# Expert stage over a list of 71 slot tiles, with weights addressed through a register, stationary tokens and three places for weights

## Chip, cores and metric

The kernel runs on one core of one Trainium2 chip. The metric is the time of one execution on the device, in microseconds (us), as the median of several runs.

## What is computed

4096 tokens (16 sequences of 256) of 512 features pass two gated residual blocks. The first is a recurrence over time (WKV) with the normalized tokens as keys and the context as values. The second is a mixture of experts: 8 routed experts, two for each token, and one shared MLP of hidden size 1408. The routed part:

```python
logits = x_flat @ router                       # (4096, 8)
topk_logits, sel = jax.lax.top_k(logits, 2)
cw = softmax(topk_logits)
C = 1280                                       # slots of one expert
buf[e, position of the token among those of e] = x_flat[token]    # if the position is below C
gate, up = split(einsum('ecd,edm->ecm', buf, w_up_gate), [352])   # 512 -> 2 x 352
h = silu(gate) * up
out_buf = einsum('eci,eid->ecd', h, w_down)                       # 352 -> 512
y[token] += cw * out_buf[e, position]
out = x + tanh(g_ffn) * (y + shared_mlp(x_flat))
```

Products are made in float16 with each operand split in a high and a low half, so one product is three matmuls (high x high, high x low, low x high).

## The kernel before, in words

Each engine has its own instruction stream, written out in order, and semaphores tie them together. The program has 16 *units* of 256 tokens (two tiles of 128). A unit runs in 11 steps, one for each of the 11 blocks of the shared MLP's hidden size: `up_pair` (matmuls at L930) makes the block's up projection, and `down_block` (L951) the down projection of the unit before. The attention part of later tokens is spread over the same steps by the table `STAGE_AT`: transposes on TensorE (L854), scans and reciprocals on VectorE, factors on GpSimd. Units 1 to 12 run partly in hardware loops, units 12 to 15 are written out. Each step's hidden block goes through one of three buffers (`srng`, and `PU` in PSUM), so TensorE can be three blocks ahead of VectorE. The down projections of units 13 to 15 are *held*: they run on TensorE around the expert stage (`held_down`, L1054), the first half of unit 13's ahead of it and the rest behind.

Routing runs on VectorE beside the units. `send_slots` on GpSimd (L545) writes, by indirect DMA, token number and weight of each choice into the slot table `slot_d` (10240 slots: 8 experts of 1280). The last two routes (`LAST`) come in unit 15: VectorE's `address_slots` for the last one waits (ahead of L1254) until the slots of the one before have been sent. GpSimd then reads the table back (L607), TensorE turns it (`turn_table`), and VectorE makes index lists from it (`slot_indices`, L1201 to L1203).

The expert stage then goes over all 80 slot tiles of 128 slots, filled or not, expert by expert, in *chunks* of two tiles (5 chunks for each expert), in hardware loops over pairs of experts:

- GpSimd copies an expert's indices (L617, L618), gathers the rows of each tile from `xhl_d` (L627) and, when a tile's result is staged, adds it to `moe_d` in memory by an indirect DMA with addition (L645, the scatter-add). Up to two of these are in flight; `retire` (L635) lets a staging buffer go when one has landed.
- SyncE turns gathered rows by DMA transposes (L421) and loads the next expert's weights in 11 pieces (L408, L412).
- TensorE: `up_chunk` (L1018) holds a 128 x 128 (or 128 x 96) block of weights still and streams 256 tokens, 72 matmuls for a chunk; `down_chunk` (L1032) holds tokens' hidden values still and streams 512 weight columns, 9 matmuls for a tile. The up projection of the next chunk is issued ahead of the down projection of this one.
- ScalarE: silu (L813), high half of the hidden block (L815), staging of the result with its weight (L822), high half of the next expert's weights (L800, L803). VectorE: product (L1356), low half (L1359), low half of the weights (L1344, L1348).

Two sets of weight buffers are used in turn, one in `wkv` (free after the attention part), one in `acc`. Expert 0's weights are loaded and split in unit 15. At the end SyncE waits for the scatter-adds, loads the sums of the held tiles, and copies the rest of `moe_d` to the output.

## Time and profile before

| | us |
|---|---|
| median of 3 runs | 1300.6 (1297.64 to 1302.33) |
| the profiled execution | 1298.67 |
| its span, first to last instruction | 1296.9 |
| TensorE matmuls busy | 1222.8 |
| GpSimd, VectorE, ScalarE busy | 667.9, 687.7, 542.0 |
| granted TensorE clock, mean share of full speed | 0.997 |

The profile is of one execution. PE is TensorE's matmuls, PEld its weight loads, PEldq its sequencer, DVE VectorE, ACT ScalarE, POOL GpSimd, SPq SyncE's queue. A matmul's printed duration holds the pipeline's depth as well, so a rate is read from the starts, or from how long many take together. The span starts with the first instruction; 1.8 us of the execution's time lie around it.

### The profile page before, as it was taken

What the parts mean: (1) busy time and instruction counts of PE and PEld (TensorE: products, weight loads), DVE (VectorE), ACT (ScalarE), POOL (GpSimd) and SP (SyncE); (2) the same over time, 40 slices, a digit from 0 to 9 for tenths busy, and PEclk for the clock granted to TensorE, in tenths of its full rate; (3) what the DMA queues carried; (4) which work ended last, traced back from release to release, by engine and by line L of the source; (5) the groups of instructions that cost most, each with busy time, mean ns of one, the idle gap of its engine ahead of it and who ended that gap; (6) DMA issues with size and microseconds to landing.
All of it is one profiled execution on the core that took longest, in us unless ns stands there. A gap on an engine that the chain in (4) does not pass through costs nothing.

```text
span 1296.9 us, 27395 instructions
## 1 busy us (share of the span) xinstructions
PE 1222.8 (94%) x9541; PEld 932.1 (72%) x9541; DVE 687.7 (53%) x1410; ACT 542.0 (42%) x1022; POOL 667.9 (52%) x765
## 2 busy tenths in 40 slices
PE   1579999999999999999999879999999999999998
PEld 1467777777777777777777757777777777777753
DVE  6778767777776766767768533322323232232212
ACT  5676435445344444434444423333434343343320
POOL 7888565474574573664567422444444444444320
PEclk9999999999999999999999989999999999999999
DMA  9272222122131221222111256998988888898748
GB/s 240 72 211 54 63 56 60 49 56 57 57 73 49 63 50 57 57 57 62 45 42 50 41 128 145 163 173 163 176 165 184 152 186 159 166 166 171 122 55 308
DMA packets 188148, 142.74 MB, mean 110 GB/s; under 512 B 127581, under 2 KB 151157, under 8 KB 187936
## 3 DMA queue, kind: packets, MB, share of 16 engines
q1 hardware_dynamic: 167168, 99.38, 31.5%
q0 software_dynamic: 20064, 42.19, 18.0%
q8 instruction: 56, 0.92, 0.3%
q14 instruction: 28, 0.23, 0.1%
q10 hardware_dynamic: 832, 0.02, 0.0%
HBM read 72.19 MB, written 46.81 MB: 92 GB/s over the span
## 4 chain that ended last, share of the span: by engine, by line
PE 79%; DMA 4%; DVE 3%; issue 3%; POOL 1%; ACT 1%; SPq 1%; DVEq 0%; POOLq 0%; ACTq 0%
PE PU L930 28%; PE PU L1018 22%; PE PD L951 14%; PE PD L1032 10%; PE PT L854 2%; DMA wkv<-in_L_ffn_w_up_gate 2%; SPq L421 1%; DMA moe_d<-acc 1%; PE PR L854 1%; POOL slot_d L545 1%; PE PT L1054 1%; PE PR L1054 1%; DMA acc<-moe_d 1%; DVE wkv L1153 1%; DVE srng L1188 0%
## 5 line engine op out<-in xcount | busy, mean ns | idle before, releaser
L930 PE MATMUL PU<-xT,wreg 128*128 128x256 f16 x4224 | 500.4, 273 | 3.7 <-DVE srng L1188 3.7
L930 PEld LDWEIGHTS PU<-xT,wreg 128*128 128x128 f16 x4224 | 410.8, 98 | 73.5 <-DVE srng L1188 3.2
L645 POOL DMA_INDIRECT moe_d<-acc x80 | 129.0, 1612 | 178.0 <-ACT acc L822 144.0
L951 PE MATMUL PD<-wreg,hreg 128*128 128x512 f16 x858 | 206.4, 379 | 0.0
L736 ACT ACTIVATE srng<-PU 128x256 f32<-128x256 f32 x176 | 67.0, 381 | 265.9 <-PE PU L930 243.7
L1018 PE MATMUL PU<-acc,wkv 128*128 128x256 f16 (+1 forms) x1440 | 163.1, 274 | 9.6 <-DMA acc<-xT 6.3
L1018 PEld LDWEIGHTS PU<-acc,wkv 128*128 128x128 f16 (+1 forms) x1440 | 146.9, 107 | 27.8 <-issue 8.4
L1018 PE MATMUL PU<-acc 128*128 128x256 f16 (+1 forms) x1440 | 160.9, 273 | 3.0 <-DVE acc L1356 3.0
L1018 PEld LDWEIGHTS PU<-acc 128*128 128x128 f16 (+1 forms) x1440 | 146.3, 106 | 19.1 <-DVE acc L1356 3.6
L561 POOL TENSOR_TENSOR hreg<-srng,hreg 128x256 f16<-128x256 f32 x165 | 123.0, 749 | 67.6 <-ACT hreg L752 66.2
L951 PEld LDWEIGHTS PD<-wreg,hreg 128*128 128x128 f16 x858 | 84.0, 98 | 73.5
L1188 DVE SCALAR_TENSOR_TENSOR srng<-PU,srng 128x256 f32<-128x256 f32 x176 | 73.9, 420 | 100.4 <-ACT srng L736 97.5
L1356 DVE SCALAR_TENSOR_TENSOR acc<-PU,acc 128x256 f32<-128x256 f32 (+1 forms) x120 | 50.4, 420 | 120.4 <-ACT acc L813 120.3
L1153 DVE RECIPROCAL wkv<-wkv 128x512 f32<-128x512 f32 x32 | 106.9, 3341 | 0.1
L752 ACT ACTIVATE hreg<-srng 128x256 f16<-128x256 f32 x176 | 71.9, 408 | 66.6 <-DVE srng L1188 65.0
L822 ACT ACTIVATE acc<-PD,acc 128x512 f32<-128x512 f32 x80 | 54.8, 685 | 70.9 <-PE PD L1032 41.9
L813 ACT ACTIVATE acc<-PU 128x256 f32<-128x256 f32 (+1 forms) x120 | 45.0, 375 | 88.8 <-PE PU L1018 87.1
L1032 PE MATMUL PD<-acc,wkv 128*128 128x512 f16 (+1 forms) x360 | 81.1, 379 | 0.9 <-ACT acc L822 0.9
L1359 DVE TENSOR_TENSOR wkv<-acc,wkv 128x256 f16<-128x256 f32 (+1 forms) x120 | 51.0, 425 | 57.9 <-ACT wkv L815 50.6
L1032 PE MATMUL PD<-wkv 128*128 128x512 f16 (+1 forms) x360 | 81.1, 379 | 0.0
L545 POOL DMA_INDIRECT slot_d<-stw,sidx x64 | 66.7, 1043 | 25.5 <-issue 15.8
L854 PE MATMUL PT<-ident,wkv 128*128 128x128 f32 x256 | 41.9, 289 | 40.2 <-ACT wkv L700 29.0
(140 smaller groups left out, 1364.0 us busy)
## 6 DMA issues: line engine op xcount, KB each, us to landing
wkv<-in_L_ffn_w_up_gate SPq DMA_DIRECT2D x64, 176.0 KB
acc<-in_x SPq DMA_DIRECT2D x32, 256.0 KB, 3.0
wkv<-in_ctx SPq DMA_DIRECT2D x32, 256.0 KB, 2.7
xhl_d<-wkv SPq DMA_DIRECT2D x32, 256.0 KB, 2.2
moe_d<-acc SPq DMA_DIRECT2D x13, 512.0 KB, 4.4
out<-moe_d SPq DMA_DIRECT2D x2, 3328.0 KB, 21.1
acc<-n_L_ffn_shared_w_up_gate SPq DMA_DIRECT2D x16, 256.0 KB, 5.7
wkv<-in_L_ffn_w_down SPq DMA_DIRECT2D x16, 256.0 KB
```

The costliest lines, as they stand in the source:

```text
L545: pool.indirect_dma_start(out=slot_d, out_offset=bass.IndirectOffsetOnAxis(ap=sidx[:, 2 * t + k:2 * t + k + 1], axis=0), in_=stw[:, k, t, ...
L561: pool.tensor_tensor(hh[:, u.par, m, 1, :], srng[:, r, :], hh[:, u.par, m, 0, :], ALU.subtract).then_inc(hlo_ready, 1)
L645: pool.indirect_dma_start(out=moe_d, out_offset=bass.IndirectOffsetOnAxis(ap=eidx[:, p, 1, s:s + 1], axis=0), in_=ostage[s % 2], in_offset ...
L736: act.activation(srng[:, r, :], PU[r][:, 0:UN], ACT.Silu, scale=1.0 / WS).then_inc(silu_done, 1)
L752: act.activation(hh[:, buf, m, 0, :], srng[:, r, :], ACT.Copy).then_inc(hhi_ready, 1)
L854: mm = pe.transpose(dst[:, kt * P:(kt + 1) * P], src[:, kt * P:(kt + 1) * P], ident[:, :])
L930: mm = pe.matmul(PU[r][:, gu * UN:(gu + 1) * UN], sU[:, m, gu, a, kt, :], xT[:, u.par, b, kt, :], start=(kt == 0 and a + b == 0), stop=(kt ...
L951: mm = pe.matmul(PD[t][:, :], hh[:, u.par, j, a, t * P:(t + 1) * P], sD[:, j, b, :], start=(j == 0 and a + b == 0), stop=(j == JT - 1 and ...
L1018: mm = pe.matmul(PU[r][0:M, gu * CH:(gu + 1) * CH], eU[p][:, gu, a, kt, m * P:m * P + M], xgT[:, (p + j) % 2, b, kt, :], start=(kt == 0 an ...
L1032: mm = pe.matmul(PD[t][:, :], eh[0:M, (p + j) % 2, m, a, t * P:(t + 1) * P], eD[p][0:M, m, b, :], start=(m == 0 and a + b == 0), stop=(m = ...
L1153: dve.reciprocal(nd[:, 1], nd[:, 1]).then_inc(rcp_done, 1)
L1188: dve.scalar_tensor_tensor(out=srng[:, r, :], in0=PU[r][:, UN:2 * UN], scalar=HS / WS, in1=srng[:, r, :], op0=ALU.mult, op1=ALU.mult).then ...
```

## The change

The slot tiles of the expert stage are no longer the 80 of the slot table but a list of 71 positions (8192 choices / 128 + 7). Each expert's filled tiles come at the next free positions, not before a fixed earliest one (`START`), which leaves the remaining experts their room. Unfilled positions gather a valid row and add to rows behind the tokens.

- **Making the list.** GpSimd prepares tables in `place_tables`, after its last `hidden_lo` and before the last `send_slots`. In unit 15 TensorE counts the choices (`count_all`), VectorE computes the places in 8 small dependent steps (`place_tiles`), TensorE moves each position's weight place (*home*) into a row (`place_homes`), VectorE finishes with three more (`place_experts`), and `turn_table` multiplies the slot table with the 0/1 matrix `Pm` where it had been transposed.
- **Weights.** Three homes in `acc`, expert e in home e % 3. TensorE loads the position's home from SBUF into a register (`home_at`) and addresses the weights by it. Expert 0's weights are loaded and split in unit 13, expert 1's in unit 15, the others' during the stage through four buffers (they were two), at fixed positions (`chunks_at`).
- **Up projection.** For one tile at a time the tokens are held still and 352 weight columns stream (24 matmuls). The hidden tile then has tokens in its partitions, so TensorE transposes it in three f32 transposes (`turn_hidden`), issued behind 8 matmuls of the next tile's up projection. ScalarE and VectorE make both halves from the transposed tile, one instruction each. The down projection stays at 9 matmuls of 512 columns.
- **Gather and scatter.** Indices are read where they are, without copies. A scatter-add waits until the one before has landed; three staging buffers (they were two).
- The stage is written out, without hardware loops.

```diff
+NPOS = NTOK * TOPK // P + E - 1
+START = [max(0, NPOS - ET * (E - e)) for e in range(E)]
+HOMES = 3
+EARLY = 2
+EARLY_UNIT = 13
+SMALL = 9728
...
-        ebuf = [wkv[:, 0:EW // 2].bitcast(F16), acc[:, 0:EW // 2].bitcast(F16)]
-        eU = [b[:, 0:UW].rearrange("p (g h k c) -> p g h k c", g=2, h=2, k=KT) for b in ebuf]
-        eD = [b[:, UW:EW].rearrange("p (j h c) -> p j h c", j=IT, h=2) for b in ebuf]
+        home = acc[:, 0:HOMES * EW // 2].bitcast(F16).rearrange("p (n c) -> p n c", n=HOMES)
+        eU = [home[:, n, 0:UW].rearrange("p (g h k c) -> p g h k c", g=2, h=2, k=KT) for n in range(HOMES)]
+        eD = [home[:, n, UW:EW].rearrange("p (j h c) -> p j h c", j=IT, h=2) for n in range(HOMES)]
...
+        ostage = [carve(D) for _ in range(3)]
...
+        def chunk_home(w):
+
+            if w < EARLY * WCH:
+                return w % 2, 16 * (w // 2 + 1)
+            n = w - EARLY * WCH
+            return 2 + n % 4, 16 * (n // 4 + 1)
+
+        def chunks_at(t):
+
+            n, m = divmod(t - 1, ET)
+            if not 0 <= n < E - EARLY:
+                return []
+            return [(n + EARLY, q) for q in range(WCH) if (q // 2 if q < 6 else q - 3) == m]
+
...
-            def turn_slots(e, p, j):
-                cc = EC * e + j
-                for t in range(2):
-                    r = (2 * (EC * p + j) + t) % 4
-                    wait_alone(gathered[r], 16 * (EC * pair_of(e, p) + (2 * (EC * p + j) + t) // 4 + 1))
-                    if not (isinstance(e, int) and cc < 2):
-                        wait_alone(eup_ready, IT * (cc - 1))
-                    sp.dma_start_transpose(
-                        xgT[:, (p + j) % 2, :, :, t * P:(t + 1) * P].rearrange("p h k t -> p (h k) t"), xg[r]).then_inc(turn_done(e, p, j, t)[0], 16)
+            def turn_slots(t):
+                sp.wait_ge(gathered[t % 4], 16 * (t // 4 + 1))
+                if t >= 4:
+                    wait_alone(eup_ready, t - 3)
+                sp.dma_start_transpose(xgT[:, t % 4].rearrange("p h k t -> p (h k) t"), xg[t % 4]).then_inc(xg_turned[t % 4], 16)
...
+            for t in range(NPOS):
+                if t + 4 < NPOS:
+                    turn_slots(t + 4)
+                for e, q in chunks_at(t + 2):
+                    load_chunk(e, q)
+
...
+            def place_tables():
+                ready = [0]
+
+                def keep(ins):
+                    ready[0] += 1
+                    ins.then_inc(cmade, 1)
+                    pool.wait_ge(cmade, ready[0])
+
+                pool.wait_ge(moe_started, 16 * EARLY_PARTS)
+                keep(pool.memset(sel, 1.0))
...
+                keep(pool.iota(own_tile[:, 0:E], pattern=[[ET, E]], base=0, channel_multiplier=-1,
...
+                for e in range(E - 2, -1, -1):
+                    keep(pool.affine_select(out=home_of, in_=home_of, compare_op=ALU.is_ge, fill=float(e % HOMES),
+                                            base=-ET * (e + 1), pattern=[[0, 1]], channel_multiplier=1))
+                for e in range(E):
+                    pool.memset(earliest[:, e:e + 1], float(START[e])).then_inc(cmade, 1)
+                    hi = START[e + 1] if e + 1 < E else NPOS
+                    pool.memset(no_home[:, START[e]:hi], -float(e % HOMES)).then_inc(cmade, 1)
...
                 hidden_lo(Unit(0, UNITS - 2), m)
+            place_tables()
             for r in LAST:
                 for t in range(UT):
...
+            AHEAD = 7
+            for t in range(AHEAD):
+                gather_rows(t)
+            for t in range(NPOS):
+                pool.wait_ge(ostaged, t + 1)
+                if t > 0:
+                    wait_alone(rows_added, 16 * t)
+                pool.indirect_dma_start(
+                    out=moe_d, out_offset=bass.IndirectOffsetOnAxis(ap=didx[:, t:t + 1], axis=0),
+                    in_=ostage[t % 3], in_offset=None, compute_op=ALU.add).then_inc(rows_added, 16)
+                if t + AHEAD < NPOS:
+                    gather_rows(t + AHEAD)
...
+            def expert_silu(t):
+                act.wait_ge(eup_ready, t + 1)
+                if t >= 2:
+                    act.wait_ge(eh_turned, t - 1)
+                act.activation(eh[:, t % 2, 0:I], up_set[t % 2][0][:, 0:I], ACT.Silu, scale=1.0 / WS).then_inc(esilu_done, 1)
+
+            def expert_hi(t):
+                act.wait_ge(eh_turned, t + 1)
+                act.activation(ehT[:, t % 2, 0, :], PR[:, 0:IT * P], ACT.Copy).then_inc(ehhi_ready, 1)
+
+            def stage_out(t):
+                act.wait_ge(edown_ready, t + 1)
+                if t >= 3:
+                    act.wait_ge(rows_added, 16 * (t - 2))
+                act.activation(ostage[t % 3], PD[t % 2][:, :], ACT.Copy, scale=wslot[:, t:t + 1]).then_inc(ostaged, 1)
+
+            act.wait_ge(gidx_ready, 3)
+            for t in range(NPOS + 2):
+                if 1 <= t <= NPOS:
+                    expert_silu(t - 1)
+                if t >= 2:
+                    stage_out(t - 2)
+                if 1 <= t <= NPOS:
+                    expert_hi(t - 1)
+                for e, q in chunks_at(t):
+                    weights_hi(e, q)

...
+                pe.wait_ge(psteps, PSTEPS + 1)
+                pe.matmul(PR[:, 0:NPOS], tokt[:, :, 0], Pm, start=True, stop=False)
+                pe.matmul(PR[:, 0:NPOS], lane, spare, start=False, stop=True).then_inc(slots_turned, 1)
+                pe.matmul(PR[:, NPOS:2 * NPOS], tokt[:, :, 1], Pm, start=True, stop=True).then_inc(slots_turned, 1)
...
-            def up_chunk(e, p, j):
-                cc = EC * e + j
-                if j == 0:
-                    pe.wait_ge(ew_lo, WCH * (e + 1))
-                for t in range(2):
-                    pe.wait_ge(*turn_done(e, p, j, t))
...
+            def home_at(t):
+                return pe.value_load(homes[0:1, t:t + 1], min_val=0, max_val=HOMES - 1)
+
+            def weights(h, lo, rows, cols):
+                return home[0:rows, bass.ds(h, 1), lo:lo + cols].rearrange("p n c -> p (n c)")
+
+            def expert_up(t, h, between):
+                for e in range(E):
+                    if START[e] == t:
+                        pe.wait_ge(ew_lo, WCH * (e + 1))
+                pe.wait_ge(xg_turned[t % 4], 16 * (t // 4 + 1))
+                if t >= 2:
+                    pe.wait_ge(eh_ready, t - 1)
+                done = 0
+                for gu in range(2):
+                    for kt in range(KT):
+                        for a, b in ((0, 0), (0, 1), (1, 0)):
+                            if done == 8:
+                                between()
+                            mm = pe.matmul(up_set[t % 2][gu][:, 0:I], xgT[:, t % 4, a, kt, :],
+                                           weights(h, ((gu * 2 + b) * KT + kt) * I, P, I),
+                                           start=(kt == 0 and a + b == 0), stop=(kt == KT - 1 and a == 1))
+                            done += 1
+                mm.then_inc(eup_ready, 1)
+
+            def turn_hidden(t):
+                pe.wait_ge(eh_ready, t + 1)
+                if t > 0:
+                    pe.wait_ge(ehlo_ready, t)
                 for m in range(IT):
+                    mm = pe.transpose(PR[:, m * P:(m + 1) * P], eh[:, t % 2, m * P:(m + 1) * P], ident[:, :])
+                mm.then_inc(eh_turned, 1)
+
+            def expert_down(t, h):
+                pe.wait_ge(ehlo_ready, t + 1)
+                if t >= 2:
+                    pe.wait_ge(ostaged, t - 1)
+                for m in range(IT):
                     M = IM[m]
+                    for a, b in ((0, 0), (0, 1), (1, 0)):
+                        mm = pe.matmul(PD[t % 2][:, :], ehT[0:M, t % 2, a, m * P:(m + 1) * P],
+                                       weights(h, UW + (m * 2 + b) * D, M, D),
+                                       start=(m == 0 and a + b == 0), stop=(m == IT - 1 and a == 1))
+                mm.then_inc(edown_ready, 1)
...
+            h = home_at(0)
+            expert_up(0, h, lambda: None)
+            for t in range(1, NPOS):
+                g = home_at(t)
+                expert_up(t, g, lambda: turn_hidden(t - 1))
+                expert_down(t - 1, h)
+                h = g
+            turn_hidden(NPOS - 1)
+            expert_down(NPOS - 1, h)
...
+            def place_tiles():
+                dve.wait_ge(cmade, CMADE)
+                dve.memset(counts[:, 0:1], 0.0)
+                wait_alone(counts_ready, 1)
+                pstep(1, dve.tensor_tensor(filled, PL[0:E * ET, 0:E].unsqueeze(2).to_broadcast([E * ET, E, ET]),
+                                           multiples.unsqueeze(1).to_broadcast([E * ET, E, ET]), ALU.is_gt))
...
+                pstep(8, dve.tensor_scalar(Pm, places, place[:, 0:1], None, ALU.is_equal))
+
+            def place_experts():
+                dve.wait_ge(homes_turned, 2)
+                pstep(9, dve.tensor_scalar(spare, PL[0:1, E + NPOS:E + 2 * NPOS], 1.0, -1.0, ALU.subtract, ALU.mult))
+                pstep(10, dve.scalar_tensor_tensor(out=no_home, in0=PL[0:1, E + NPOS:E + 2 * NPOS], scalar=1.0, in1=no_home,
+                                                  op0=ALU.subtract, op1=ALU.mult))
+                dve.tensor_tensor(homes, PL[0:1, E:E + NPOS], no_home, ALU.add).then_inc(homes_ready, 1)

...
+            def expert_hidden(t):
+                dve.wait_ge(esilu_done, t + 1)
+                dve.scalar_tensor_tensor(out=eh[:, t % 2, 0:I], in0=up_set[t % 2][1][:, 0:I], scalar=HS / WS,
+                                         in1=eh[:, t % 2, 0:I], op0=ALU.mult, op1=ALU.mult).then_inc(eh_ready, 1)
+
+            def expert_lo(t):
+                dve.wait_ge(ehhi_ready, t + 1)
+                dve.tensor_tensor(ehT[:, t % 2, 1, :], PR[:, 0:IT * P], ehT[:, t % 2, 0, :], ALU.subtract).then_inc(ehlo_ready, 1)
+
+            for t in range(NPOS + 1):
+                if t >= 1:
+                    expert_hidden(t - 1)
+                    expert_lo(t - 1)
+                for e, q in chunks_at(t):
+                    weights_lo(e, q)

```

TensorE's stream around the start of one chunk, before. ISA and REGISTER_ALU are register instructions of its sequencer; PU holds up projections, PD down projections:

```order
L1012 ISA [waits xg_turned01,xg_turned00]
L1018 MATMUL PU<-acc,wkv 128x256 [waits eh_ready]
L1018 MATMUL PU<-acc,wkv 128x256 x23
L1018 MATMUL PU<-acc,wkv 128x256 [waits eh_ready]
L1018 MATMUL PU<-acc,wkv 128x256 x23
L1012 REGISTER_ALU
L1018 MATMUL PU<-acc,wkv 96x256 [waits eh_ready]
L1018 MATMUL PU<-acc,wkv 96x256 x23
L1028 REGISTER_ALU [waits ehlo_ready]
L1032 MATMUL PD<-wkv 128x512 [waits ostaged]
L1032 MATMUL PD<-wkv 128x512 x8
```

And around one tile of the changed kernel. PR takes the transposed hidden tile, TENSOR_LOAD is the load of the home:

```order
L1047 TENSOR_LOAD wkv
L1047 ISA x2
L1065 ISA [waits eh_ready,xg_turned2]
L1065 MATMUL PU<-acc,wkv 128x352
L1065 ISA
L1065 MATMUL PU<-acc,wkv 128x352 x2
...
L1065 MATMUL PU<-acc,wkv 128x352
L1076 MATMUL PR<-ident,wkv 128x128 [waits ehlo_ready,eh_ready]
L1076 MATMUL PR<-ident,wkv 128x128 x2
...
L1086 ISA [waits ehlo_ready]
L1086 MATMUL PD<-acc,wkv 128x512
L1086 ISA
L1086 MATMUL PD<-acc,wkv 128x512 x2
```

A tile's up projection has a load, then register instructions between nearly all matmuls; the down projection's first register instruction waits for `ehlo_ready`, where before a REGISTER_ALU did so ahead of 18 matmuls.

GpSimd's stream around the last slots (L545 is `send_slots`, L607 the read back), before:

```order
L561 TENSOR_TENSOR hreg<-srng,hreg 128x256 [waits hhi_ready] x6
L545 DMA slot_d<-stw,sidx 18432x2 [waits rsteps]
L545 DMA slot_d<-stw,sidx 18432x2 x3
L545 DMA slot_d<-stw,sidx 18432x2 [waits rsteps]
L545 DMA slot_d<-stw,sidx 18432x2 x3
L607 DMA wkv<-slot_d 80x256 [waits slots_sent]
```

And now, where L582 is `send_slots`, in front of it `place_tables`:

```order
L598 TENSOR_TENSOR hreg<-srng,hreg 128x256 [waits hhi_ready] x6
L637 MEMSET acc 80x8 [waits moe_started]
L638 AFFINE_SELECT acc<-acc 80x8 [waits cmade]
L640 AFFINE_SELECT acc<-acc 80x8 [waits cmade]
L642 IOTA acc 80x8 [waits cmade]
...
L650 MEMSET acc 80x1 [waits cmade]
L652 AFFINE_SELECT acc<-acc 80x1 [waits cmade] x7
L655 MEMSET acc 80x1 [waits cmade]
L657 MEMSET acc 1x1
...
L582 DMA slot_d<-stw,sidx 18432x2 [waits rsteps]
L582 DMA slot_d<-stw,sidx 18432x2 x3
```

Between the last `hidden_lo` (L598) and the first of the last sends there are now 33 instructions of `place_tables`.

## Rows read from the trace of the kernel before

**Rows 1.** The page, busy us of each engine, share of the span, instructions.
```profile
PE 1222.8 (94%) x9541; PEld 932.1 (72%) x9541; DVE 687.7 (53%) x1410; ACT 542.0 (42%) x1022; POOL 667.9 (52%) x765
```

**Rows 2.** Busy times by stretch: us, PE, PEld, DVE, ACT, POOL, clock, DMA share, GB/s.
```profile
647.40:693.40 46.00, 46.00 (x374) 35.31 (x372) 32.52 (x75) 21.14 (x36) 25.55 (x36) 1.00 0.18 41
774.00:1249.00 475.00, 468.37 (x3576) 360.64 (x3577) 139.97 (x317) 180.16 (x394) 202.12 (x166) 1.00 0.84 160
```

**Rows 3.** The chain of waits in the expert stage: start us, us, what.
```profile
821.26 7.86 PE PU L1018 x72
829.12 3.89 PE PD L1032 x18
...
844.76 7.86 PE PU L1018 x72
```

**Rows 4.** Timeline at the start of the stage, TensorE, then GpSimd: start us, us, what.
```profile
774.26 15.07 PE L1018 MATMUL PU<-acc,wkv 128*128 128x256 f16 x120 [6.25 <-DMA acc<-xT]
...
763.26 0.19 POOL L617 COPY acc<-acc 128x10 uint32<-128x10 uint32 x1 [12.42 <-DVE acc L1203]
...
764.67 1.02 POOL L627 DMA_INDIRECT xT<-xhl_d,acc  x1 [0.89 <-POOL acc L618]
```

**Rows 5.** Its end: TensorE's timeline, and the chain of waits.
```profile
1251.41 4.05 PE L1032 MATMUL PD<-acc,wkv 128*128 128x512 f16 x18 [0.87 <-ACT acc L822]
...
1259.88 5.41 DMA moe_d<-acc
```

**Rows 6.** TensorE's timeline in the attention part.
```profile
595.31 0.60 PE L854 MATMUL PT<-ident,wkv 128*128 128x128 f32 x4
595.74 0.49 PE L930 MATMUL PU<-xT,wreg 128*128 128x256 f16 x3
```

**Rows 7.** Groups in the stage, one form each: busy us, mean ns, idle before.
```profile
L800 ACT ACTIVATE acc<-wkv 128x352 f16<-128x352 f32 x32 | 15.7, 492 | 34.9 <-DMA wkv<-in_L_ffn_w_up_gate 31.3 <-issue 3.2
L1344 DVE SCALAR_TENSOR_TENSOR acc<-wkv,acc 128x352 f16<-128x352 f32 x32 | 16.8, 525 | 69.5 <-ACT acc L800 52.8 <-issue 16.4
```

**Rows 8.** TensorE's sequencer (PEldq), by line: ns min/median/max, first and last start us.
```profile
L1006 PEldq EVENT_SEMAPHORE  x1: 51/51/51, 840.8 to 840.8; - x1
L1012 PEldq FUSED_REGOPS  x1: 51/51/51, 840.9 to 840.9; - x1
...
L918 PEldq EVENT_SEMAPHORE  x1: 51/51/51, 50.3 to 50.3; - x1
...
L881 PEldq EVENT_SEMAPHORE  x1: 51/51/51, 50.6 to 50.6; - x1
...
L1063 PEldq COMPARE_BRANCH  x1: 3804/3804/3804, 901.2 to 901.2; - x1
...
905.44 0.55 PEld L1018 LDWEIGHTS PU<-acc,wkv 128*128 128x128 f16 x6 [0.85 <-issue]
```

**Rows 9.** One scatter-add on GpSimd's timeline, and the line behind its landing.
```profile
952.66 1.59 POOL L645 DMA_INDIRECT moe_d<-acc  x1 [4.47 <-ACT acc L822]
...
L635 POOLq EVENT_SEMAPHORE  x1: 17/17/17, 957.6 to 957.6; - x1
```

**Rows 10.** GpSimd's timeline at the start of the program.
```profile
1.98 0.29 POOL L478 TENSOR_SCALAR_AFFINE_SELECT srng<-srng 128x128 f32<-128x128 f32 x1
2.34 0.40 POOL L480 CAST pref<-srng 128x256 f16<-128x256 f32 x1
2.81 0.14 POOL L481 IOTA iotae<- 128x8 f32 x1
3.02 0.16 POOL L483 IOTA rowid<- 128x32 f32 x1
```

**Rows 11.** Timelines of GpSimd, VectorE and TensorE around the last slots.
```profile
730.95 1.07 POOL L545 DMA_INDIRECT slot_d<-stw,sidx  x1 [0.16 <-issue]
...
738.43 0.17 DVE L1254 COPY stw<-rowid 128x2 f32<-128x2 f32 x1 [3.25 <-DMA slot_d<-stw,sidx]
...
741.57 8.04 PE L930 MATMUL PU<-xT,wreg 128*128 128x256 f16 x72 [2.18 <-DVE srng L1188]
```

380 lines of the change are left out of this document (151 added, 229 removed).

## Prediction

> **What bounds the kernel now.** The page's busy times come first [rows 1]: TensorE is busy for 94% of the span, at full clock, every other engine for about half. The busy times of each stretch [rows 2] then show where the expert stage lies: from 774 to 1249 us TensorE is busy for 468 of 475 us, ScalarE and VectorE for 180 and 140, GpSimd for 202, and the DMA engines' share is 0.84, against 0.18 in a unit ahead of it. The chain of waits inside the stage [rows 3] is nothing but TensorE: 72 up matmuls of 256 columns in 7.86 us, 18 down matmuls of 512 columns in 3.89 us, again and again. So one matmul costs 109.2 ns at 256 columns and 216.1 ns at 512, and two slot tiles cost 11.75 us, one 5.875. Forty such pairs are 470 us; the stage runs from 774.26 to 1251.41 + 4.05 = 1255.46 [rows 4, 5], 481.2 us, so 11.2 us of it are gaps. Behind it TensorE works on the held down projections, so what the stage gains or loses in TensorE's time reaches the end nearly in full.
>
> **The stage, per tile.** The line through 109.2 and 216.1 ns gives 0.4176 ns a column, and 149.3 ns for 352. A tile now has 24 up matmuls of 352 columns, 3.58 us (before 4.61 for 36 of 256), and 9 down matmuls, 1.945 us, as before. New are three f32 transposes of the hidden tile. Four such, in the attention part, start at 595.31 and the next work at 595.74 [rows 6], 0.108 us each, so 0.325 us. Sum 5.85 us, times 71 tiles 415.4 us. The last tile has no other up projection beside its transposes: transposes, ScalarE's copy, VectorE's subtraction and wake-ups stand open, about 1.6 us. I add 2 us for jitter of transfers: 419.0 against 481.2, which is **-62.2 us**. Nine tiles fewer are 53 us of it, the rest is the old gaps.
> A row of transposes by the Trainium skill ("TensorE: Matmul & The Clock Gate", Part 4: PE-mode transpose) costs more: it states about 275 ns for one in a kernel's context, which would put 0.5 us on each tile and the end at 1278 us. The duration printed for one here is 272 ns, but the starts are 0.108 us apart, so they overlap, and the row decides.
>
> **What runs beside it.** In a tile's time, counted from its first up matmul: the transposes of the tile before are issued behind 8 matmuls, at 1.19, and done by about 1.7. ScalarE's copy of 384 columns comes from 0.492 us at 352 [rows 7] to some 0.53, VectorE's subtraction from 0.525 at 352 [rows 7] to 0.55, wake-ups about 0.1 each: the low half stands at about 3.05. The down matmuls need it at 0.325 + 3.58 = 3.9. Silu and the product (0.49 and 0.53 by the 352-column rows) fit in the 1.95 us of the down matmuls ahead. ScalarE works about 2.7 us of 5.85 with two weight chunks, VectorE 2.1. This costs nothing while the margin of 0.85 us holds.
>
> **The register.** Every tile has one load of the weights' home into a register of TensorE's sequencer, and 26 other control instructions. The sequencer works ahead of the array: at 840.9 it did the register work of the chunk whose matmuls start at 844.76 [rows 3, 8]. Control instructions start 0.1 us apart there [rows 8]; 18 pairs of weight load and matmul were passed on between 50.3 and 50.6 [rows 8], under 0.02 us each. 26 x 0.105 + 36 x 0.015 = 3.3 us of 5.85, plus the load. But the sequencer now stops for the low half of the hidden tile. From 3.05 it needs the wake-up, 5 register instructions and 9 pairs, to 3.8; then the load; then 4 control instructions and the first weights, 0.5. The array runs dry at 5.85, so a load of up to about **1.5 us is free**, and above it each tile takes 4.3 us plus the load. No row shows such a load. Below stands another register instruction, 0.05 us [rows 8]; above the branch at the end of the loop body, 3.80 us, of which 0.85 us showed as idle time of the weight loads [rows 8]. I take 1 us, nearer to the register instruction, since it moves one word. At 3.8 us the tile would take 8.1.
> Two pages of the Trainium skill give a price: about 600 ns ("DMA: Bandwidth & Descriptors", Latency and other measured facts) and about 1.3 us ("Runtime: NRT & Kernel Launch", The ~15µs preamble/postamble breakdown). By either the load stays hidden and the sum is the same.
>
> **The scatter.** Before, two scatter-adds were in flight; now each waits for the one before. One takes 4.9 us to landing inside the stage (from 952.66 to the semaphore work at 957.6) and 5.41 in the tail [rows 5, 9]. With 0.4 us to the next start that is a period of 5.3 to 5.8, just under 5.85. The issue of 1.59 us and a gather's of about 1 fit in it. Three staging buffers take up single late ones. I cost it at nothing beyond the 2 us.
> Transfers per tile stay the same and so does the pace, so the DMA share stays near 0.84 [rows 2].
>
> **Ahead of the stage.** GpSimd builds the tables of the placement before it sends the last slots: 9 selects of 0.36 us start to start, 5 iotas of 0.21 [rows 10], and 19 memsets, which I put at 1.7 us together, 6 us in all (5 to 8). It had started the sends at 730.95; VectorE waited for them until 738.43, and TensorE for VectorE until 741.57 [rows 11]. None of these three has slack, so **+6.0 us**. Expert 0's weights move into unit 13, where TensorE is busy 46.0 of 46.0 us and VectorE 32.5 [rows 2]: 6 us more on VectorE and ScalarE have room (bounds 0 and 5 us). The 11 small VectorE steps of the placement, 0.3 us each, fall in unit 15, where three buffers stand ahead of TensorE (0 to 3.4). I take **+1 us** for both. The first expert matmul waited for two gathers and two transposes, behind index copies that took from 763.26 to the first gather at 764.67 [rows 4]: now no copies (1.4 us) and one tile instead of two (another 1 us), **-2.4 us**.
>
> **Behind it.** The last scatter landed at 1259.88 + 5.41, 9.8 us after the last down matmul [rows 5], and the sums are loaded behind it beside 36 us of held projections. Now it should land about 7 us after. No change.
>
> Sum against the profiled execution: 1298.7 - 62.2 + 6.0 + 1.0 - 2.4 = 1241.1. The median of the runs is 1.9 us above that execution, so the forecast for the median is **1243 us**.
>
> **Rivals.**
> *A. The sequencer shows (0.20).* The load takes over 1.5 us, or the low half comes later than 3.9. For: the sequencer stops once per tile, and matmuls whose address comes from a register, of which the trace has none, may be passed on more slowly than 0.015 us a pair. Against: 1.5 us of room. At 2.0 us the tile takes 6.3, at 2.5 us 6.8: 1275 to 1310, and below 1296 it still counts as faster.
> *B. The scatter chain binds (0.14).* If the mean latency is 5.8 us, not 4.9 to 5.4, a tile takes 6.2: 1268 us; at 6.1, 6.5 and 1289. For: the DMA engines are at 0.84 [rows 2]. Against: both rows are quicker, and they had a second scatter in flight beside them.
> *C. The array is drained for each load (0.16): slower.* One mechanism: the load of tile t+1 is not done ahead but only when the down matmuls of tile t are through. Then the load, the control instructions behind it and the first weights, 1.6 us at a load of 1 us, stand open in each tile: 7.45 us, 1357. It decides from 6.65 us a tile on, where the gain of 57 us is gone. For: the trace holds no such load, and so nothing that says it may run ahead. Against: the branch of 3.80 us began at 901.2 [rows 8] inside a down block, so that control instruction did not wait for the array.
> *D. The placement does not shorten anything (0.02).* 71 is a fixed count, so nine tiles do go; only the front could cost more.
>
> **Numbers.** Forecast 0.48 (1236 to 1252), A 0.20, B 0.14, C 0.16, D 0.02. Faster by over 0.3% (3.9 us, about what a measurement of this kernel tells from none): 0.48 + 0.14 + 0.18 of A, 0.80; within 0.3%: 0.01 of A and 0.02 of D, 0.03; slower: 0.16 of C and 0.01 of A, 0.17. The range leaves out C, the top of A and little below: 1232 to 1298.
>
> **What would show it.** Up matmuls of 352 columns start 149 ns apart, and down blocks end 5.85 us apart; no idle time of the matmuls between the down block and the next up block. If A: idle time put down to issue just there. If B: ScalarE's staging copy waits for the scatter's landing, and TensorE for ScalarE. If C: the idle time is over 0.8 us per tile. The wait of VectorE for slots lasts 9 us, not 3.3. I am wrong if the stage, from first to last expert matmul, is not within 416 to 428 us.

## The result and the profile after

The changed kernel takes **1296.6 us** (median of 19 runs, 1282.1 to 1305.3), the kernel before 1299.3 us (19 runs, 1297.6 to 1302.3) in the same comparison. The ratio is 0.9946, interval 0.9922 to 0.9971: faster by 0.5%, where 4.4% was forecast. The ratio leaves out four executions of the changed kernel that lie more than 1.5% above its fastest; the medians of all 19 differ by 0.2% only. The number lies just inside the range, 54 us above the forecast. The executions of the changed kernel also spread over 23 us, those of before over 5.

| us | before | forecast | after |
|---|---|---|---|
| first expert matmul starts | 774.3 | 778.9 | 790.5 |
| expert stage | 481.2 | 419.0 | 451.2 |
| from the last expert matmul to the end of the span | 41.4 | 41.4 | 50.1 |
| span | 1296.9 | 1239.3 | 1291.8 |
| the profiled execution | 1298.7 | 1241.1 | 1293.5 |

So the stage did give 30 us, and the two ends took 25 back. The page's busy times, and the busy times of the stage and of what follows it (columns as in [rows 2]):

```profile
PE 1187.5 (92%) x8506; PEld 829.6 (64%) x8506; DVE 666.3 (52%) x1325; ACT 507.7 (39%) x915; POOL 642.5 (50%) x764
```

```profile
790.50:1241.70 451.20, 429.37 (x2557) 256.87 (x2558) 109.30 (x208) 142.45 (x278) 175.75 (x135) 0.98 0.81 148
1241.70:1292.00 50.30, 38.23 (x166) 16.54 (x164) 7.93 (x12) 0.69 (x1) 4.65 (x3) 0.90 0.71 217
```

In [rows 2] TensorE was busy for 468.4 of 475 us of the stage. Now it is for 429.4 of 451.2, at a mean granted clock of 0.98, and behind the stage at 0.90. TensorE bounds the stage only in part; the reader's first question is what it waits for.

**The tile itself came as forecast.** TensorE's timeline, one tile from down block to down block:

```profile
847.31 2.11 PE L1086 MATMUL PD<-acc,wkv 128*128 x9
849.25 1.36 PE L1065 MATMUL PU<-acc,wkv 128*128 x8
850.45 0.49 PE L1076 MATMUL PR<-ident,wkv 128*128 128x128 f32 x3
850.77 2.55 PE L1065 MATMUL PU<-acc,wkv 128*128 x16
853.16 2.11 PE L1086 MATMUL PD<-acc,wkv 128*128 x9
```

853.16 - 847.31 is 5.85 us, the forecast to the hundredth. Of the 70 distances between the tiles' transposes 43 are 5.85 us, 8 are 5.91, and the last, which has no other up projection in it, is 4.66; the other 18 hold 31 us more than 5.85 each. Three transposes stand 0.33 us from the next matmul, so a transpose costs 0.11 us, as in [rows 6]. The 275 ns that the Trainium skill ("TensorE: Matmul & The Clock Gate", Part 4: PE-mode transpose) states (for bf16; these are f32) were not seen as a cost of each. The register load, on TensorE's sequencer (duration in ns, smallest, median, largest, then first and last start):

```profile
L1047 PEldq TENSOR_LOAD <-wkv x69: 297/307/1293, 800.2 to 1229.6; - x69
```

0.30 us in the median, once 1.29: nearer to the register instruction of 0.05 than the 1 us I took. The Trainium skill's floor of about 600 ns ("DMA: Bandwidth & Descriptors", Latency and other measured facts) is twice the measured median; the 1.3 us that the prediction named beside it are stated for several registers loaded from HBM, another case. The sequencer stays ahead of the array: the load at 841.2 lies beside the down block in front of its tile.

**What the stage waits for.** TensorE's waits, then ScalarE's, each summed over the stage (us in total, times, longest):

```profile
PE PR L1076 <- DVE wkv L1445: 20.2, 15, 3.7
```

```profile
ACT acc L832 <- DMA wreg<-in_L_ffn_w_up_gate: 56.1, 17, 6.8
ACT acc L835 <- DMA wreg<-in_L_ffn_w_down: 42.5, 12, 6.9
ACT wkv L864 <- DMA moe_d<-wkv,acc: 19.6, 10, 4.3
```

TensorE waits for VectorE's product, that for ScalarE's silu, and ScalarE stands 98.6 us behind weight chunks that SyncE brought late. Where these come from is seen by following one wait back. GpSimd, SyncE, ScalarE and TensorE between 1001 and 1018 us (L698 is the scatter-add, L687 the gather, L466 the token transpose, L415 a chunk of down weights, L835 and L854 the chunk's high half and silu, L1076 the transposes of the hidden tile):

```profile
1001.67 1.89 POOL L698 DMA_INDIRECT moe_d<-wkv,acc  x1 [4.20 <-issue]
1003.87 0.98 POOL L687 DMA_INDIRECT wkv<-xhl_d,acc  x1 [0.30 <-issue]
1008.31 1.58 POOL L698 DMA_INDIRECT moe_d<-wkv,acc  x1 [3.46 <-issue]
```

```profile
1008.34 1.27 SPq L466 DMA_TRANSPOSE wkv<-wkv  x1
1009.66 0.57 SPq L415 DMA_DIRECT2D wreg<-in_L_ffn_w_down  x1
```

```profile
1015.59 0.63 ACT L835 ACTIVATE acc<-wreg 128x512 f16<-128x512 f32 x1 [6.06 <-DMA wreg<-in_L_ffn_w_down]
1016.13 0.45 ACT L854 ACTIVATE wkv<-PU 128x352 f32<-128x352 f32 x1
```

```profile
1017.44 0.90 PE L1076 MATMUL PR<-ident,wkv 128*128 128x128 f32 x3 [2.90 <-DVE wkv L1445]
1018.13 1.38 PE L1065 MATMUL PU<-acc,wkv 128*128 x4
```

Scatter 31 starts at 1001.67, but scatter 32 only at 1008.31, 6.64 us later, since it waits for the landing. Gather 38 is issued behind scatter 31, at 1003.87, and lands at 1008.2. SyncE turns those tokens at 1008.34, and only then issues a weight chunk, at 1009.66, which lands at 1015.57. ScalarE stood before it for 6.06 us with the silu behind it. TensorE loses 2.90 us, and then works at half its clock for 2.6 us (the granted clock of 1017.4 to 1020.0 is 0.50, the level of 1.2 GHz): three transposes take 0.90 us instead of 0.49, four matmuls 1.38 instead of 0.76. So every link of this chain goes back to the scatter-add, though its own name hardly appears among the waits. Its line:

```profile
L698 POOL DMA_INDIRECT moe_d<-wkv,acc x71: 1547/1582/1916, 803.6 to 1255.2; - x71
DMA to landing us min/median/max: 4.6/5.5/7.5
```

The first starts at 803.6 and the 71st at 1255.16, so 70 periods are 451.6 us, **6.45 us each** against TensorE's 5.85. By the starts and landings of all 71, a landing takes 5.54 us on average (4.6 to 7.5), and from it to the next start it is 0.82 us wherever nothing else is late.

**The end.** The last down block, the wait of the held projections for the sums, and the last scatter-add:

```profile
1239.73 2.12 PE L1086 MATMUL PD<-acc,wkv 128*128 x9 [1.51 <-DVE wkv L1450]
...
1271.79 9.59 PE L1100 MATMUL PT<-wreg,hreg 128*128 128x512 f16 x33 [8.57 <-DVE acc L1286]
```

```profile
1255.16 4.71 DMA moe_d<-wkv,acc
```

The last result was staged at 1244, but its scatter-add had to queue behind two others and started at 1255.16. The sums were loaded behind it, TensorE stood still for 8.57 us, and its next 33 matmuls took 9.59 us instead of 7.29 (the granted clock is 0.50 from 1266.2 to 1276.5).

**The front.** GpSimd's timeline: the last `hidden_lo`, the first table, the first of the last sends, the first gather; VectorE's copy behind the sends; TensorE behind VectorE and at the first expert matmul:

```profile
741.28 0.67 POOL L598 TENSOR_TENSOR hreg<-srng,hreg 128x256 f16<-128x256 f32 x1 [0.51 <-ACT hreg L795]
741.89 0.10 POOL L637 MEMSET acc<- 80x8 f32 x1
...
747.16 1.09 POOL L582 DMA_INDIRECT slot_d<-stw,sidx  x1 [0.34 <-issue]
...
781.61 1.28 POOL L687 DMA_INDIRECT xT<-xhl_d,acc  x1 [14.57 <-DVE acc L1255]
```

```profile
753.70 0.17 DVE L1333 COPY stw<-rowid 128x2 f32<-128x2 f32 x1 [7.42 <-DMA slot_d<-stw,sidx]
```

```profile
757.04 2.10 PE L960 MATMUL PU<-xT,wreg 128*128 128x256 f16 x9 [6.49 <-DVE srng L1239]
...
790.50 7.23 PE L1065 MATMUL PU<-acc,wkv 128*128 x32 [4.20 <-DMA wkv<-xT]
```

[Rows 11] had the first send at 730.95, [rows 4] the first gather at 764.67. The sends are 16.2 us late, of which the tables are 4.9 (741.89 to the end of the last memset at 746.8) and 11.2 us stood there already: the last `hidden_lo` starts at 741.28, and did so at 730.12 before. Most of this comes from unit 13, as experiment 3 shows. SyncE, ScalarE, VectorE and TensorE there (L412 is a chunk of expert 0's weights, L832 and L1424 its halves, L884 a transpose of the attention part):

```profile
663.67 0.58 SPq L395 DMA_DIRECT2D xhl_d<-wkv  x1
664.30 13.23 SPq L412 DMA_DIRECT2D acc<-in_L_ffn_w_up_gate  x5
```

```profile
667.45 0.50 ACT L832 ACTIVATE acc<-acc 128x352 f16<-128x352 f32 x1 [4.89 <-DMA acc<-in_L_ffn_w_up_gate]
```

```profile
667.98 0.53 DVE L1424 SCALAR_TENSOR_TENSOR acc<-acc 128x352 f16<-128x352 f32 x1 [3.62 <-ACT acc L832]
```

```profile
672.88 1.12 PE L884 MATMUL PT<-ident,wkv 128*128 128x128 f32 x4 [3.72 <-DVE wkv L1207]
```

The chunk is issued at 664.30, behind the tokens' transpose and store of the same step. ScalarE, VectorE and then TensorE stand behind it, 4.89, 3.62 and 3.72 us.

### The profile page after: what moved, and what is told of

Same layout as the page of the kernel before. It is cut to its first block and busy times, and to the rows that moved or that the text cites. A ratio compares the mean times of both kernels' runs of the same rounds, so it can differ in the third digit from the quotient of the medians.

```text
span 1291.8 us, 25674 instructions
## 1 busy us (share of the span) xinstructions
PE 1187.5 (92%) x8506; PEld 829.6 (64%) x8506; DVE 666.3 (52%) x1325; ACT 507.7 (39%) x915; POOL 642.5 (50%) x764
## 5 line engine op out<-in xcount | busy, mean ns | idle before, releaser
L698 POOL DMA_INDIRECT moe_d<-wkv,acc x71 | 114.6, 1615 | 265.7 <-issue 178.5
L1065 PE MATMUL PU<-acc,wkv 128*128 x1284 | 222.0, 320 | 4.2 <-DMA wkv<-xT 4.2
L1065 PEld LDWEIGHTS PU<-acc,wkv 128*128 128x128 f16 x1284 | 127.9, 100 | 78.0 <-issue 4.7
L598 POOL TENSOR_TENSOR hreg<-srng,hreg 128x256 f16<-128x256 f32 x165 | 122.1, 743 | 71.3 <-ACT hreg L795 69.9
L1086 PE MATMUL PD<-acc,wkv 128*128 (+1 forms) x639 | 149.7, 379 | 1.5 <-DVE wkv L1450 1.5
L1450 DVE TENSOR_TENSOR wkv<-PR,wkv 128x384 f16<-128x384 f32 x71 | 39.6, 557 | 169.6 <-ACT wkv L858 142.9
L1086 PEld LDWEIGHTS PD<-acc,wkv 128*128 128x128 f16 (+1 forms) x639 | 62.5, 98 | 68.0 <-issue 1.9
L884 PE MATMUL PT<-ident,wkv 128*128 128x128 f32 x256 | 42.5, 292 | 44.9 <-ACT wkv L743 29.0
L864 ACT ACTIVATE wkv<-PD,acc 128x512 f32<-128x512 f32 x71 | 48.6, 685 | 77.6 <-PE PD L1086 57.9
L582 POOL DMA_INDIRECT slot_d<-stw,sidx x64 | 66.3, 1037 | 25.3 <-issue 16.0
L570 POOL TENSOR_TENSOR wkv<-wkv 128x512 f32<-128x512 f32 x32 | 44.4, 1388 | 59.9 <-DVE wkv L1191 59.9
L1065 PE MATMUL PL<-acc,wkv 128*128 x420 | 69.9, 317 | 0.0
L884 PEld LDWEIGHTS PT<-ident,wkv 128*128 128x128 f32 x256 | 32.1, 149 | 55.2 <-ACT wkv L743 31.3
```

Source lines behind the costliest of these rows:

```text
L582: pool.indirect_dma_start(out=slot_d, out_offset=bass.IndirectOffsetOnAxis(ap=sidx[:, 2 * t + k:2 * t + k + 1], axis=0), in_=stw[:, k, t, ...
L598: pool.tensor_tensor(hh[:, u.par, m, 1, :], srng[:, r, :], hh[:, u.par, m, 0, :], ALU.subtract).then_inc(hlo_ready, 1)
L698: pool.indirect_dma_start(out=moe_d, out_offset=bass.IndirectOffsetOnAxis(ap=didx[:, t:t + 1], axis=0), in_=ostage[t % 3], in_offset=None, ...
L884: mm = pe.transpose(dst[:, kt * P:(kt + 1) * P], src[:, kt * P:(kt + 1) * P], ident[:, :])
L1065: mm = pe.matmul(up_set[t % 2][gu][:, 0:I], xgT[:, t % 4, a, kt, :], weights(h, ((gu * 2 + b) * KT + kt) * I, P, I), start=(kt == 0 and a ...
L1086: mm = pe.matmul(PD[t % 2][:, :], ehT[0:M, t % 2, a, m * P:(m + 1) * P], weights(h, UW + (m * 2 + b) * D, M, D), start=(m == 0 and a + b = ...
```

## The experiments

Theory **S** is that the single scatter-add in flight paces the stage, with 5.54 us to landing and 0.82 to the next start. Its rival **Q** is that the order of SyncE's queue makes the weights late, whatever the scatter-adds do. For the front, theory **F** is that expert 0's chunks are loaded too late, and its rival **G** that the added work of these chunks costs the time by itself. Theory **T** is that the tables stand on the path of the last sends. All ratios are to the kernel before, run beside.

**1. Two scatter-adds in flight.** Two positions of the same expert hold different tokens, so their scatter-adds cannot meet in a row; only at a change of expert, or where a position is unfilled, must one wait. VectorE makes a row of 0 and 1 from the homes, GpSimd loads it into a register, and two semaphores take turns:

```diff
-                if t > 0:
-                    wait_alone(rows_added, 16 * t)
+                if t >= 3:
+                    wait_alone(rows_added[t % 2], 16 * (t // 2))
+                    wait_alone(rows_added[(t - 1) % 2], new[t] * 16 + 16 * ((t - 1) // 2))
+                elif t > 0:
+                    for k in range(t):
+                        wait_alone(rows_added[k % 2], 16 * (k // 2 + 1))
...
+                dve.tensor_tensor(pace[:, 1:NPOS], homes[:, 1:NPOS], homes[:, 0:NPOS - 1], ALU.not_equal).then_inc(homes_ready, 1)
+                wait_alone(homes_ready, 2)
+                dve.tensor_tensor(pace[:, 1:NPOS], pace[:, 1:NPOS], spare[:, 1:NPOS], ALU.max).then_inc(homes_ready, 1)
```

> Change: two scatter-adds may be in flight where the position and the one before it belong to the same expert (or the pair is marked safe); at the change of expert and at unfilled positions the wait stays. Two semaphores take turns. Theory S (the chain of single scatter-adds binds the stage: 5.54 us to landing on average and 0.82 us to the next start, 6.45 us a position against TensorE's 5.855): the stage falls from 451 us to 416 to 422, TensorE's 20 us of waits and the low clock behind them go, the last scatter-add lands about 8 us after the last down matmul and not 18, the 8.6 us wait for the sums goes: 1247 to 1258 us in all. Theory Q (the order of SyncE's queue delays the weight chunks, whatever the scatter does): waits of ScalarE for weights stay, stage above 440 us, 1280 us or more.

Measured: 1251.5 us (1250.4 to 1256.2), ratio 0.966 (0.963 to 0.968). TensorE's timeline, first expert matmul and held blocks, and the scatter-add's line:

```profile
788.85 7.18 PE L1075 MATMUL PU<-acc,wkv 128*128 x32 [4.33 <-DMA wkv<-xT]
...
1208.55 7.29 PE L1110 MATMUL PR<-wreg,hreg 128*128 128x512 f16 x33
1215.67 14.41 PE L1110 MATMUL PD<-wreg,hreg 128*128 128x512 f16 x66
1229.92 7.29 PE L1110 MATMUL PT<-wreg,hreg 128*128 128x512 f16 x33
```

```profile
L708 POOL DMA_INDIRECT moe_d<-wkv,acc x71: 1546/1575/1664, 801.9 to 1212.2; - x71
```

The stage is 1208.55 - 788.85 = 419.7 us (forecast of the change: 419.0), the held blocks follow without a wait, and the scatter-adds keep TensorE's pace, 410.3 us for 70. A landing takes 5.16 us on average here. ScalarE's waits for weight chunks in the stage, 98.6 us before this edit, are gone, though SyncE's queue has its old order. S holds, Q falls as the cause. The wait at a change of expert stays for a reason that is not measured here: the Trainium skill ("DMA: Bandwidth & Descriptors", Two DMAs through the same engine are not ordered) says of two read-modify-writes of one row that the second may read old data. No run here shows that, since none lets them meet.

**2. Weight chunks ahead of the token transposes in SyncE's queue.**

```diff
-                if t + 4 < NPOS:
-                    turn_slots(t + 4)
                 for e, q in chunks_at(t + 2):
                     load_chunk(e, q)
+                if t + 4 < NPOS:
+                    turn_slots(t + 4)
```

> Change: in the stage SyncE issues a position's weight chunks ahead of the token transpose of the same position; one scatter-add in flight as in the changed kernel. Theory S: the waits move from the weight chunks to the tokens or the staging buffers, the stage stays at 445 us or more, 1288 to 1300 us. Theory Q: the stage falls to about 420 us, 1255 to 1268 us.

Measured: 1297.9 us (1287.5 to 1308.3), ratio 0.9993 (0.9960 to 1.0025). ScalarE's waits in the stage:

```profile
ACT wkv L864 <- DMA moe_d<-wkv,acc: 178.3, 51, 6.7
ACT acc L832 <- DMA wreg<-in_L_ffn_w_up_gate: 22.7, 14, 3.6
```

Weights cost 22.7 us of waiting now and not 98.6, and the staging buffer 178.3 instead of 19.6. A period of the scatter-adds stays at 6.45 us. The wait has changed its name and the time has stayed: the late weights had only passed on a delay that the scatter-adds made.

**3. Expert 0's chunks loaded a step ahead, before the token transpose.**

```diff
+                    if also is not None and s + 1 < JT:
+                        also(s + 1)
                     for v, k in tiles_at("split_x", u, s):
                         turn_and_store(v, k)
...
-                    if also is not None:
-                        also(s)
...
+                    load_chunk(0, 0)
                 unit(Unit(0, v), 0, (lambda q: load_chunk(0, q)) if v == EARLY_UNIT else None)
```

> Change: in unit 13 SyncE loads each weight chunk of expert 0 one step ahead, and ahead of the token transpose, instead of behind it in the step that uses it. Theory F (ScalarE and VectorE stand still behind a chunk that is loaded too late, and with them TensorE): VectorE's waits of 3.6 and 4.5 us for the chunks at 668 and 692.6 us go, and the first expert matmul comes at 779 to 782 us, not 790.5; total 8 to 11 us less. Rival G (it is the added work of the chunks itself): at most 3 us less.

Measured: 1286.0 us (1276.4 to 1299.1), ratio 0.992 (0.990 to 0.994). GpSimd's last `hidden_lo`, and the first expert matmul:

```profile
733.34 0.67 POOL L599 TENSOR_TENSOR hreg<-srng,hreg 128x256 f16<-128x256 f32 x1 [0.51 <-ACT hreg L796]
```

```profile
783.15 7.49 PE L1066 MATMUL PU<-acc,wkv 128*128 x32 [4.25 <-DMA wkv<-xT]
```

`hidden_lo` comes 7.9 us sooner and the first expert matmul 7.4. That is less than the 8.5 to 11.5 us expected for the first expert matmul: 3.2 of the 11.2 us remain (against 730.12 before). The total, for which 8 to 11 us less were expected, is 10.5 less by the medians and 4 by the ratios (0.992 against 0.9946), since the executions spread over 23 us; experiments 1 and 5 show it better. F holds for the larger part. The rest may be the chunks' work itself, as G had it; it was not tested apart.

**4. The kernel before with a single scatter-add in flight.**

```diff
                     wait_alone(ostaged, ET * e + s + 1)
+                    if s >= 1:
+                        retire(s - 1)
                     pool.indirect_dma_start(
...
-                    if s >= 1:
-                        retire(s - 1)
```

> The kernel before, with one scatter-add in flight: each waits until the one before has landed. Theory S: the period is 5.4 us to landing and 0.8 to the next start, 6.2 to 6.3 us a tile against TensorE's 5.875, so the stage grows from 481 to 497 to 505 us and the total to 1315 to 1325 us. If the single flight costs nothing: 1299 us, within 4.

Measured: 1350.0 us (1341.3 to 1351.7), ratio 1.038 (1.034 to 1.043). The scatter-add's line:

```profile
L647 POOL DMA_INDIRECT moe_d<-acc x80: 1549/1586/2089, 797.5 to 1311.9; - x80
DMA to landing us min/median/max: 4.6/5.0/8.4
```

Slower by 52 us, and twice what was expected. From the first to the 80th start it is 514.4 us, 6.51 each and not 6.2 to 6.3: 5.35 to landing, mostly 0.92 to the next start (0.1 more than I took), and now and then up to 4.9; the average is 1.16. The profile names ScalarE's staging as what ended GpSimd's idle time ahead of 11 of these scatter-adds, so there the result was late. Why it was late was not tested. S holds in a kernel with none of the other edits; its price was too low, as in the forecast.

**5 and 6. The repairs together.** First the edits of 1 and 3; then with them `place_tables()` in unit 14, ahead of the `hidden_lo` for which GpSimd waits 5.06 us:

```diff
+                    if u.fixed and u.v == UNITS - 2 and s == 10:
+                        place_tables()
...
-            place_tables()
             for r in LAST:
```

> Two scatter-adds in flight, and expert 0's weight chunks loaded a step ahead. If the two faults are independent (F: the front ends 7.4 us sooner, and with S repaired nothing behind gives it back): 7 to 8 us under the 1251.5 of the first alone, 1243 to 1245 us. If the front's gain is swallowed by the scatter chain or by the last experts: 1248 or more.

> As before it, and GpSimd builds the placement's tables in unit 14, ahead of the hidden block for which it waits 5.06 us, instead of ahead of the last sends. Theory T (the 5.0 us of tables stand on the path of the last sends): VectorE's wait for the sent slots falls from 7.4 back to about 3.3 us, the first expert matmul comes 4.5 to 5.2 us sooner, 1238 to 1240 us in all. If other work sets that point: no change against the run without it.

Measured: 1243.7 us (1240.5 to 1246.0), ratio 0.959 (0.957 to 0.962), and with the tables moved **1239.3 us** (1237.9 to 1240.9), ratio 0.9555 (0.9530 to 0.9579). Of the second, VectorE's copy behind the sends, the first expert matmul, and the busy times of the stage:

```profile
741.31 0.17 DVE L1349 COPY stw<-rowid 128x2 f32<-128x2 f32 x1 [2.95 <-DMA slot_d<-stw,sidx]
```

```profile
777.82 6.59 PE L1077 MATMUL PU<-acc,wkv 128*128 x32 [4.34 <-DMA wkv<-xT]
```

```profile
777.80:1196.90 419.10, 417.58 (x2556) 254.87 (x2557) 109.39 (x208) 143.42 (x278) 176.23 (x137) 1.00 0.91 160
```

By the medians the early chunks give 7.8 us more on top of experiment 1, and the tables another 4.4. VectorE's wait for the sent slots is 2.95 us again, 7.62 in the fifth experiment, so T holds. The first expert matmul comes only 3.4 us sooner than in the fifth (781.25), not the 4.5 to 5.2 expected, and the first 32 take 6.59 us where they took 4.94 there. The stage is 419.1 us, at a mean granted clock of 1.00. This version beats both kernels: 4.5% under the kernel before, and its runs lie within 3 us.

**7. The three edits and the order of experiment 2.**

> The three edits, and in the stage SyncE issues the weight chunks ahead of the token transposes. Theory S: with two scatter-adds in flight nothing is late in SyncE's queue, so within 1.5 us of the kernel without it. Theory Q: a further 3 us or more less.

Measured: 1239.9 us (1239.5 to 1240.3), against 1239.3: no difference. With the scatter chain repaired the order of SyncE's queue is worth nothing.

**8. The three edits with the home as a constant.**

```diff
-                return pe.value_load(homes[0:1, t:t + 1], min_val=0, max_val=HOMES - 1)
+                return max(e for e in range(E) if START[e] <= t) % HOMES
```

> The three edits, with the weights' place a constant of the program at each position instead of a register loaded from SBUF: no load and no register instructions on TensorE's sequencer. It leaves out the choice of the right expert where an expert's tiles come ahead of the latest position possible, so those tiles use another expert's weights. Forecast of the register (0.30 us a load, 3.3 us of other control instructions, all beside the array's work): within 1.5 us of the kernel with registers. Rival A or C: 5 us or more less.

Measured: 1241.6 us (1238.6 to 1242.5), if anything 2.3 us above the kernel with registers, which is more than the 1.5 expected and the wrong way for a gain; with four runs each that spread over 3 to 4 us I call it none. The register costs nothing that shows here: A or C would have made this kernel 5 us faster or more.

**9. Fewer bytes beside the scatter-adds.**

```diff
-                    sp.dma_start(wst[r][:, 0:I], w_ug[e, k * P:(k + 1) * P, g * I:(g + 1) * I]).then_inc(ew_in[r], 16)
+                    n = I if w < EARLY * WCH + 4 else 16
+                    sp.dma_start(wst[r][:, 0:n], w_ug[e, k * P:(k + 1) * P, g * I:g * I + n]).then_inc(ew_in[r], 16)
```

> The changed kernel with one scatter-add in flight, but from the fifth weight chunk of the stage on only 16 of a chunk's columns are transferred. It leaves out the weights of the experts 2 to 7, so their tiles use old ones; every wait and every instruction stays. Theory S with its cause (a scatter-add lands later the more bytes of others move beside it): landing falls from 5.54 to 4.9 to 5.1 us, and with 0.82 us a position takes 5.75 to 5.9 us, so that TensorE's 5.855 sets the pace: stage 418 to 426 us, 1253 to 1265 us. If the landing does not hang on the other transfers: stage 445 us or more, 1285 us or more.

Measured: 1282.1 us (1275.4 to 1286.8), ratio 0.990 (0.985 to 0.994). The scatter-add's landings:

```profile
DMA to landing us min/median/max: 4.6/5.1/6.7
```

14 us less by the medians, 6 by the ratios, where 32 to 44 were expected. The mean landing fell from 5.54 to 5.28 us only, a period from 6.45 to 6.18. So the weights' bytes are at most a small part of what makes a landing long, up to a quarter of a microsecond. Even that is not firm: in experiment 3, with all the bytes, the profiled execution has 5.41 and 6.31. What the rest is stays open. Gathers and token transposes were still there. For the last six positions, behind the last gather, a landing took 4.5 to 5.0 us in each profile with addition and one scatter-add in flight.

**10. The scatter without the addition.**

```diff
-                    in_=ostage[t % 3], in_offset=None, compute_op=ALU.add).then_inc(rows_added, 16)
+                    in_=ostage[t % 3], in_offset=None).then_inc(rows_added, 16)
```

> The changed kernel, its scatter a plain write instead of an addition: it leaves out the sum with what memory holds. If the read of the old sums is what makes the landing long: 1 us or more less on each, the chain falls under 5.855 us a position, 1250 to 1262 us. If it is not: landing within 0.3 us of 5.54, 1285 to 1300 us.

Measured: 1251.7 us (1249.6 to 1253.5), ratio 0.963 (0.959 to 0.967). The scatter's line, to be held against the one of the changed kernel above (duration of the issue in ns):

```profile
L698 POOL DMA_INDIRECT moe_d<-wkv,acc x71: 962/987/1183, 806.0 to 1214.4; - x71
```

A plain write lands 2.8 us from its start (median of the 71; the mean is 2.9), half of the 5.5 us with the addition, and its issue takes 0.99 instead of 1.58 us. With 0.82 us to the next start that would be a period of 3.7 us, an estimate, and TensorE sets the pace: a period is 5.83 us here. The addition is what makes the chain longer than a tile. The Trainium skill ("DMA: Bandwidth & Descriptors", Anatomy of one DMA) gives 2.0 us and the bytes by 436 GB/s, by which I estimate 2.6 us for the 262144 bytes here: the plain write comes near that, and with the addition a landing is about twice as long.

**11. A fourth staging buffer.**

```diff
-        ostage = [carve(D) for _ in range(3)]
+        ostage = [carve(D) for _ in range(4)]
```

> The changed kernel with four staging buffers instead of three, one scatter-add in flight. Theory S (the chain's rate sets the stage, not single late landings): no more than 6 us less, what one more position of slack is worth once; 1288 to 1300 us. If single late landings were the fault, as I had put it in the prediction (three buffers take them up): 1265 us or less.

Measured: 1293.7 us (1287.6 to 1306.6), ratio 0.997 (0.994 to 1.001), 3 us under the changed kernel by the medians and above it by the ratios (0.9946 there): no difference. A period stays at 6.42 us. A deeper buffer does not help against a rate.

## Why the prediction was wrong

The forecast was 1241.1 for the profiled execution, the result 1293.5. The 52.4 us split as the table does: 11.6 in front, 32.2 in the stage, 8.7 behind it. My sign of being wrong, a stage outside 416 to 428 us, came with 451.2. That 1296.6 still lies inside the range is luck: rival B, whose mechanism this is, was priced at 1289 us at most, and the room above that was there for rival A, which did not happen. Step by step:

- **Tile on TensorE, 5.85 us: right**, and with it matmuls, transposes, ScalarE's and VectorE's parts beside them, and the last tile's open 1.6 us (measured 2.0 from its transposes to its down block, 1.51 of it idle). The 4.61 us given for a tile's up matmuls before is a slip: 36 times 109.2 ns are 3.93 us, and with 1.945 that is the 5.875 of the rows. The sum does not use it.
- **The register, hidden up to 1.5 us: right.** The load is 0.30 us and its removal gives nothing (experiment 8). Neither A nor C, 0.36 together, happened.
- **"I cost it at nothing beyond the 2 us", of the scatter: this is the step that failed**, worth 32.2 us in the stage and 8.7 behind it, of 52.4. I had written a period of 5.3 to 5.8, just under 5.85; it measured 6.45. Both terms were read too low. The landing was taken from two rows, 4.9 and 5.41; the mean of the 80 in the trace before is 5.39, with single ones up to 7.3, and in the changed kernel 5.54. The way to the next start was put at 0.4 us and is 0.82. With 5.39 and 0.82 the sum would have been 6.2 us before any tail, over 5.85, and rival B the likeliest case. B named the mechanism (0.14, and 1289 us at 6.5 us a tile); "three staging buffers take up single late ones" was no answer to a rate.
- **Behind the stage, "no change": wrong, by the same cause.** A chain that is slower than TensorE ends later than TensorE: the last scatter-add landed 18 us behind the last down block, not 7, and the 36 us of held projections did not cover that and the load of the sums.
- **"6 us more on VectorE and ScalarE have room", for expert 0's weights in unit 13: wrong.** I priced the work (+1 us with the placement steps) and not the transfer in front of it. In truth it was 11.2 us up to the last `hidden_lo`, 7.9 of it for a chunk that is issued behind a token transpose in the step that needs it (experiment 3). I had the bounds 0 and 5 from busy times; a wait for a transfer has no row among busy times.
- **The tables, +6.0 us: nearly right**, 4.9 measured. When they were moved (experiment 6), 4.4 came back by the medians and 3.4 at the first expert matmul.
- **Start of the first tile, -2.4: wrong, 0.** From the first of the last sends to the first gather it is 34.5 us, before 33.7, and then 8.9 to the first matmul, before 9.6. The turned table was there at about 776.6, but VectorE came to it at 780.8, behind a weight chunk of expert 1.
- What I said would show B (ScalarE waits for the landing, TensorE for ScalarE) was seen in 19.6 us only; the rest was one step removed, behind late weights.
- **"The DMA share stays near 0.84": wrong.** At the forecast's pace, in experiment 6, it is 0.91, with the same 160 GB/s as before. Without the addition (experiment 10) it is 0.64 at 160 GB/s, so the additions keep the DMA engines busy; why the share is higher than with the 80 tiles is open.

## What to carry to other kernels

A chain with one transfer in flight has a rate of its own: landing plus the way to the next start, from the mean of all its rows, not from two of them. Where that comes as near to the compute period as 5.3 to 5.8 us did to 5.85, count it as the bound, and count what it leaves unfinished at the end of the stage. When an engine waits for a transfer, follow the issue of that transfer back through its queue before the wait's name is believed; and when work moves to an earlier place, its load has to move one step further.

## What was not expected of the hardware

- An indirect DMA of 128 rows of 2 KB with addition lands after 4.5 to 5.0 us with little beside it, 5.5 on average in the stage, up to 8.4 (experiment 4); without addition after 2.8 us. The addition adds about as much as the plain write takes in all.
- The kernels with a single scatter-add in flight had uncertain times: the changed kernel spread over 23 us in 19 executions, experiment 3 over 23 in six, the kernel before with one in flight over 10 in four. With two in flight, or without the addition, four executions spread over 1 to 6 us. That slow landings make the spread is my reading; it was not tested.
- A register load from SBUF on TensorE's sequencer took 0.30 us in the median, 1.29 at most, and ran ahead of the array's matmuls.
- After 4.20 us of idling the first 32 expert matmuls took 7.23 us (granted clock 0.50 up to 795), in the fifth experiment after 3.34 us only 4.94. After 2.90 us of idling at 1017 they were slow for 2.6 us. In these rows a wait on TensorE cost up to 2.3 us more than its own length.
